# Opening block 0 with token halves: the 72-row slot and the first convolution unit around the transposes of tiles 2 and 3

## What is computed

```python
xn = layernorm(x)
proj = einsum("bld,pd->blp", xn, in_proj_w)     # gate 4096, x 4096, B 1024, C 1024, dt 64 rows
conv = causal depthwise convolution of x, B, C over 4 tokens, then silu
dt   = softplus(dt + dt_bias);  A = -exp(A_log)
scan over tokens: state = state*exp(dt*A) + dt*x (outer) B;  y = state . C
y    = groupwise rmsnorm(y + x*D) * norm_weight * silu(gate)
out  = x + y @ out_proj_w.T + (xn @ W_base.T + b_base + routed LoRA of xn, top 2 of 8)
```

## Time and profile before

| what | us |
|---|---|
| median of 3 executions | 3192.64 |
| lowest, highest | 3192.55, 3195.68 |
| span of the profiled execution, first to last instruction | 3192.9 |
| PE busy | 3175.7 (99%) |
| DVE busy | 2256.7 (71%) |
| ACT busy | 1548.4 (48%) |
| POOL busy | 829.9 (26%) |

### The profile page before, as it was taken

How to read it: one execution, slowest core, us unless ns; L and a number is a source line. 1 busy time by engine, 2 the same in 40 slices (tenths; PEclk the granted TensorE clock), 3 DMA queues, 4 the chain that set the end, 5 groups by cost and what they waited for, 6 DMA issues and landing times.

```text
span 3192.9 us, 55463 instructions
## 1 busy us (share of the span) xinstructions
PE 3175.7 (99%) x18080; PEld 2616.4 (82%) x18080; DVE 2256.7 (71%) x4101; ACT 1548.4 (48%) x3816; POOL 829.9 (26%) x917
## 2 busy tenths in 40 slices
PE   8999999999999999999999999999999999999999
PEld 7878888887888888888888888888878888888887
DVE  7977777786587677777548767777755877776773
ACT  5666666663355444444235545444423545444441
POOL 4444434343032222222103222222210212122220
PEclk9999999999999999999999999999999999999999
DMA  7777777776655555556465555555556655555554
GB/s 288 279 256 263 267 274 266 269 267 245 239 207 185 186 185 191 185 187 206 157 236 200 188 182 186 191 184 192 192 171 233 204 182 186 189 190 193 182 187 159
DMA packets 185669, 672.66 MB, mean 211 GB/s; under 512 B 21056, under 2 KB 22208, under 8 KB 185408
## 3 DMA queue, kind: packets, MB, share of 16 engines
q1 hardware_dynamic: 161280, 584.91, 52.7%
q10 hardware_dynamic: 24128, 84.42, 7.6%
HBM read 532.41 MB, written 136.84 MB: 210 GB/s over the span
## 4 chain that ended last, share of the span: by engine, by line
PE 97%; DVE 2%; issue 0%; DMA 0%; ACT 0%; POOL 0%; ACTq 0%; SPq 0%; DVEq 0%; POOLq 0%
PE dense L1038 27%; PE dense L1040 27%; PE dense L1039 27%; PE pY L1136 3%; PE pD L1166 2%; PE pD L1136 1%; PE pX L1108 1%; PE dense L1075 1%; PE pU L1038 1%; PE pS L1040 1%; PE pCB L1113 1%; PE pS L1038 1%; PE pS L1039 1%; PE pU L1040 1%; PE pU L1039 1%; DVE conv_us L1448 1%
## 5 line engine op out<-in xcount | busy, mean ns | idle before, releaser
L1038 PE MATMUL dense<-xn_hi,w_hl 128*128 128x512 f32 (+1 forms) x2888 | 1143.9, 396 | 1.2 <-ACT conv_us L702 0.8
L1040 PE MATMUL dense<-xn_hi,w_hl 128*128 128x512 f32 (+1 forms) x2888 | 1125.2, 390 | 0.0
L1039 PE MATMUL dense<-xn_lo,w_hl 128*128 128x512 f32 (+1 forms) x2888 | 1123.4, 389 | 0.0
L1040 PEld LDWEIGHTS dense<-xn_hi,w_hl 128*128 128x128 f32 (+1 forms) x2888 | 540.1, 187 | 116.3
L1038 PEld LDWEIGHTS dense<-xn_hi,w_hl 128*128 128x128 f32 (+1 forms) x2888 | 540.7, 187 | 114.4 <-issue 2.9
L1039 PEld LDWEIGHTS dense<-xn_lo,w_hl 128*128 128x128 f32 (+1 forms) x2888 | 540.9, 187 | 110.9 <-issue 1.9
L1448 DVE SCALAR_TENSOR_TENSOR conv_us<-conv_in,const_g,conv_us 128x512 f32<-128x512 f32 x576 | 466.5, 810 | 164.0 <-ACT conv_us L683 150.3
L1038 PE MATMUL dense<-z_hi,w_hl 128*128 128x512 f32 x1024 | 406.7, 397 | 2.5 <-DVE acc L1588 2.0
L1588 DVE TENSOR_TENSOR acc<-acc,dense 128x512 f32<-128x512 f32 x256 | 175.7, 687 | 322.3 <-PE dense L1040 312.0
L1040 PE MATMUL dense<-z_hi,w_hl 128*128 128x512 f32 x1024 | 400.0, 391 | 0.0
L1039 PE MATMUL dense<-z_lo,w_hl 128*128 128x512 f32 x1024 | 399.6, 390 | 0.0
(11 more groups left out here) (202 smaller groups left out, 4427.6 us busy)
## 6 DMA issues: line engine op xcount, KB each, us to landing
w_hl<-w_split SPq DMA_DIRECT2D x732, 512.0 KB, 3.5
w_split<-w_hl SPq DMA_DIRECT2D x244, 512.0 KB, 3.6
cum_b<-cum_scratch ACTq DMA_DIRECT2D x128, 512.0 KB, 4.9
w_raw<-w_slots_dram SPq DMA_DIRECT2D x122, 512.0 KB, 5.2
acc<-x_tr_dram ACTq DMA_DIRECT2D x16, 512.0 KB, 6.9
out_tr_dram<-acc ACTq DMA_DIRECT2D x16, 512.0 KB, 4.7
BC<-x_tok_dram SPq DMA_DIRECT2D x6, 512.0 KB, 4.6
conv_us<-x_tok_dram SPq DMA_DIRECT2D x6, 512.0 KB, 5.7
```

Source lines behind the costliest of these rows:

```text
L1038: nc.tensor.matmul(out, lhs[0], rhs[0], start=start, stop=False)
L1039: nc.tensor.matmul(out, lhs[0], rhs[1], start=False, stop=False)
L1040: return nc.tensor.matmul(out, lhs[1], rhs[0], start=False, stop=stop)
```

## The change

PE's order at the start of block 0 is changed. Before: the transposes of tiles 0 to 3, the 72-row slot's first and second token half, the first convolution unit over 512 tokens. After: the transposes of tiles 0 and 1, the 72-row slot on tokens 0 to 255, the transposes of tiles 2 and 3, the first unit on tokens 0 to 255, the 72-row slot on tokens 256 to 511, the first unit on tokens 256 to 511. The first unit's 24 matmuls of 512 columns become 48 of 256 columns, and its two counts in `dense_done` now both come behind its last matmul. DVE makes the low parts of tile 1 ahead of applying tile 3. The programs of ACT, POOL and SP are as they were.

```diff
@@ PE, ahead of block_body @@
-            for i in range(NC):
-                ln_transpose(0, i, xn_first, ln_banks_first)
-
@@ PE, in block_body @@
+                def first_unit_half(first_tile, end_tile):
+
+                    cols = slice(first_tile * 128, end_tile * 128)
+                    for h in range(2):
+                        weights(0, K_FIRST, h)
+                        for t in range(4 * h, 4 * h + 4):
+                            mm = three(bank[1][:, cols], w(K_FIRST, t), (xn_hi[:, t, cols], xn_lo[:, t, cols]),
+                                       t == 0, t == KD - 1)
+                    return mm
+
                 pe.wait_ge(evac_dve, q * DVE_EV + (-1 + CR_EVAC))
                 if first_block:
+                    for i in range(2):
+                        ln_transpose(0, i, xn_first, ln_banks_first)
                     dt_slot(0, NC // 2)
+                    for i in range(2, NC):
+                        ln_transpose(0, i, xn_first, ln_banks_first)
+                    pe.wait_ge(evac_dve, q * DVE_EV + (0 + CR_EVAC))
+                    first_unit_half(0, NC // 2)
                     dt_slot(NC // 2, NC).then_inc(dense_done, 2)
+                    first_unit_half(NC // 2, NC).then_inc(dense_done, 2)
...
-                    in_unit(0, K_FIRST + j, (1 + j) % 2)
+                    if j > 0 or not first_block:
+                        in_unit(0, K_FIRST + j, (1 + j) % 2)
@@ DVE @@
             ln_low(0, 0, ln_banks_first)
+            ln_low(0, 1, ln_banks_first)
             ln_apply_first(3)
-            for i in range(1, NC):
+            for i in range(2, NC):
                 ln_low(0, i, ln_banks_first)
```

## The result

The changed kernel takes 3199.18 us (median of 18 runs, 3197.87 to 3200.02), the kernel before, run beside it, 3193.30 us (18 runs, 3191.57 to 3195.68). The ratio is 1.0017, with a 95% interval of 1.0011 to 1.0024: 5.9 us slower, 3.5 to 7.7 us by the interval. Forecast were 3199.0 us, 6.4 above the median of before that was known then (3192.64), and a range of 3195.5 to 3202.0.

What follows compares the result with a forecast made beforehand. PE, carrying 97% of the chain, was taken as the bound. PE's 4.0 plus 0.75 gave 4.7, plus 1.7 for the clock 6.4 on the 3192.9 span: 3199.3, or 3199.0 against the median; range 3195.5 to 3202.0.

Steps and rivals of the forecast that it cites:

- First half at 14.2: PE starts the 72-row slot's first token half at 14.2 us, after idling 2.05 us for DVE's low part.
- The wait for slot 1: Before the first unit's first half, PE idles 2.9 us because ACT's split of slot 1 follows tile 3's copies.
- PE's delay of 4.0 at the high level: At the high clock level the first unit ends at 30.1 us instead of 26.14, 4.0 later.
- The clock, one low stretch of 1.7: Of two possible 1.2 GHz stretches at the start, each costing 1.7 us, one was taken.
- rival A: Two low clock stretches, under the 72-row half and behind the second hole, 3.4 us: 3200.7 by the median; chance 0.20.
- ACT behind the first unit, 0.75: With both counts at the unit's end, ACT's split and copies come later, adding 0.75 us for the convolution taps.
- Rival C, the later hole: PE's hole at 165.4 to 167.4 us swallows the delay, up to 3.7 us back: 3193.6 by the median; chance 0.10.
- D, the rule that transposes don't count toward the clock: Whole first 72-row half at half pace, 2.8 us more, plus one low stretch: 3201.8 by the median; chance 0.07.
- The base: The profile's span of 3192.9 us, taken as 0.3 above the median of the runs of before.

Runs made afterwards that it cites:

- the holes filled: Changed kernel plus unused identity transposes, 9 before the 72-row half and 24 before the first unit's first half; 3196.14 us against 3192.74, ratio 1.0011.
- the second profile of before: Kernel before, unchanged, profiled once more: profiled execution 3192.82 us, span 3191.0; median 3192.74 us, ratio 0.9999.
- the changed kernel with load first: Changed kernel with SP's load of the next raw slot issued ahead of the second half's store, all through block 0; 3198.94 us against 3192.25, ratio 1.0020.
- the first profile of before: Kernel before, unchanged, the profile the prediction was made from: span 3192.9 us, execution of 3195.68 us.
- The pure delay: Kernel before plus 72 unused identity transposes ahead of the 72-row slot, 7.8 us; 3198.07 us against 3192.86, ratio 1.0017.
- another delay of 2.2: Kernel before with only DVE's low parts of tile 1 moved ahead of applying tile 3; 3193.87 us against 3192.25, ratio 1.0002.
- mending that wait: Kernel before with SP's raw-slot load issued ahead of the second store only from about 145 us on; 3190.33 us against 3192.25, ratio 0.9991.
- one count per half: Changed kernel with slot 1's two counts in dense_done one behind each half in the last token half; 3198.19 us against 3192.74, ratio 1.0017.
- the split first: Changed kernel with ACT's split of slot 1 ahead of the copies of tiles 2 and 3; 3195.05 us against 3192.74, ratio 1.0006.

## Why the prediction was right, and where only its end was

The time came out 0.2 us from the forecast, and the mechanisms named for the loss are shown. That it came so near is luck in part: the difference to the kernel before was 5.9 us for 6.4, the median of before that it was added to was 0.7 too low (3192.64 for 3193.30), and inside the sum terms cancel too.

- **First half at 14.2.** 14.16. Right, and so is the hole (1.83 us by the profile, for 2.05).
- **The wait for slot 1, 2.9 us, set by ACT's order.** 2.79 us. With the split moved ahead it is gone. Right; it is the step that carries the answer.
- **PE's delay of 4.0 at the high level.** With the holes filled the unit ends 30.66 - 26.14 = 4.5 us later, or 4.4 against the second profile of before. Right within 0.5.
- **The clock, one low stretch of 1.7.** There were two: the 72-row half ran 15 matmuls at 0.213 us and a second low stretch followed at 24.4. Filling both holes gave 2.8 us back. The start went as rival A, which had 3.4 for the two. In the changed kernel with load first only the first was there, over all 24 matmuls, so how many there are and how long is a matter of the execution, if the order of the loads has no part in it.
- **ACT behind the first unit, 0.75.** The mechanism is there, copies 1.31 us behind the end for 0.73; 0.5 us more than PE's delay reached the first chunk (7.77 for 7.28), or 1.0 against the second profile of before (8.17 for 7.17). But counting the halves apart gave 0.14 at the chunk, not 0.75: DVE's chain had a second bound, POOL's work on a raw slot that landed late, that the prediction didn't see.
- **Rival C, the later hole.** It was given 0.10 as a rival to the forecast, and it came true beside it. The hole went from 2.00 to 0, and 3.8 us came back against the first profile of before, which has a low stretch behind the hole, 2.2 against the second, which has none. The pure delay returned 7.4 - 5.1 = 2.3 at that place by its profile. One of the prediction's own signs of being wrong was the delay at 68 us no longer found at 175 us, and a quarter to a half of it was gone. I had argued that each load follows PE: its issue does, to 0.01 us, but its landing does not.
- **D, the rule that transposes don't count toward the clock.** The half ran at the full pace behind nine filler transposes and slowly behind a hole. In both profiles of before the transposes went from one in 0.21 us to one in 0.11 with nothing but transposes ahead of that. The Trainium skill's rule ("TensorE: Matmul & The Clock Gate", Part 4: PE-mode transpose) doesn't hold for these fp32 transposes. A half wholly at the low pace, as D had it, did come once, in the changed kernel with load first, so that alone would not have told D from A.
- **The base.** I set span and time equal within 0.3 us. They lie 1.7 to 3.0 apart, 2.8 in the profiled execution of before, which was a long one. That it couldn't be the median's could be seen from its three times. Against the second profile the sum is 4.4 for PE, 2.8 for the clock, 1.0 for DVE's chain, less 2.0 for the hole: 6.2, where the profiles differ by 6.1 and the medians by 5.9.

So the step that was mis-sized at the start is the clock (2.8 for 1.7), and the one left out of the sum is the later hole (-2.0); with what PE and DVE's chain had more than the sum (0.4 and 0.3) they nearly cancel. One thing stays open: why the same two stores and one load take 9.05 us in the kernel before and 6.55 to 6.87 in the later ones. The transfer that ends the hole was found, and moving it one place ahead in its queue ends the hole; which of its neighbours it loses to was not measured, nor whether the time would move in other executions of the same kernel beyond the two profiled.

## What to carry to other kernels

When work is moved on one engine, read the list of the engines that serve it: here ACT's unchanged order put a weight split behind copies that the move had made late, and a slot that had been ready 3 us ahead of its use became the bound. A hole in TensorE is to be priced with what its clock does behind it, which added 2.8 us to the 4.6 of these two. And a delay is not added up to the end by itself: look along the chain for the next wait on a transfer. Here it took 2.2 of 8.3 us back, and nothing of another delay of 2.2, and mending that wait gave the only kernel whose profile and median were both shorter than those of before.

## What the runs showed of the hardware

- Behind the same hole of 2.00 us at 165 us the granted clock was 0.50 in one profile of before and 1.00 in the other. Behind a hole of 2.79 us it was 0.51 in the changed kernel; behind one of 2.80 us in that kernel with load first it was 1.00.
- One 512 KB load took 8.0 us from its issue at 153.08 to the split that waited for it, behind two stores. Issued at 152.63, ahead of one of them, its split began at 157.24. Behind the same two stores it took 5.8 us in the changed kernel (161.38 to 167.19).
- A DVE product of two 128x256 fp32 tiles took 0.42 us by itself. Where it began while POOL subtracted, it took up to 1.57 us and ended 0.27 to 0.29 us behind POOL's instruction (four cases: the changed kernel, one count per half twice, the split first). Begun 0.04 us ahead of POOL's, it took 0.42 (L1663 at 36.39, split first, with POOL's L447 at 36.43).
